# First stacks of an attention loaded inside the stage before it, its rows stored in wider transfers, and one instruction for the shift of a layer norm

## The chip, the cores and the metric

The kernel runs on one core of a Trainium2 chip. The metric is the time of one execution on the device in microseconds (us), the median of several runs. The engines are PE (matrix products), DVE (VectorE), ACT (ScalarE), POOL (GpSimd) and SP (SyncE, which here only issues transfers); each works through its own list of instructions in order and waits on semaphores for the others.

## The reference

Two transformer layers in float32 on a batch of two sequences of 1024 rows of width 512. Every part is `x = x + layernorm(part(layernorm(x)))`:

```python
x = x + _layernorm(_L0_attn_ref(_layernorm(x), Wq, Wk, Wv, Wo))   # 16 heads of 32, rotary, causal
x = x + _layernorm(_L0_ffn_ref(_layernorm(x), w_gate, w_up, w_down))        # silu(gate) * up, 2048 wide
x = x + _layernorm(_L1_attn_ref(_layernorm(x), ...))   # 16 heads, latent q (384) and kv (128), rotary on 64
x = x + _layernorm(_L1_ffn_ref(_layernorm(x), w_gate_up, w_proj))           # weights rounded to three values
```

The layer norm has no weights: `(x - m) / sqrt(v + eps)`. The kernel computes it as `x * rstd + shift` with `rstd = 1 / sqrt(v + eps)` and `shift = -m * rstd`.

## The kernel before

The work is a row of stages, each a block of its own whose engines all meet at its end. Tiles are 128 rows of width 512; there are 8 to a sequence and 16 in all. Most matrices are held as two float32r parts, a high one that ACT copies out of PSUM and a low one that DVE (or POOL) makes by subtraction.

`front_layer0` (line 698) is the first stage. It turns the three weights, normalises each tile, turns it, and multiplies it by the weights of q, k and v; the order of PE's, ACT's and DVE's work is written out by `front_order` (line 674). For q and k DVE's `rotate` (line 868) multiplies the PSUM bank by the cosines into `direct` and by the sines, crossed, into `crossed`; POOL adds the two into `turning` (line 923), PE turns that (line 808), and ACT and DVE write the two parts into `stage` (lines 840 and 901). For every two tiles SP's `store_pair` (line 753) writes `stage` to the DRAM tensor `qk_dram` in 16 transfers: two of q and k, two parts, four heads of a group, each from 32 partitions (line 760). The value rows go out tile by tile in one or two transfers of 128 partitions (lines 777 and 781).

`attention_layer0` (line 989) works head by head. For each head SP's `load_stack` (line 1027) reads `q_stack` and `k_stack`, three blocks of 32 partitions each (high, low, high for q; high, high, low for k) in four transfers, into a ring of four. The first three heads' loads are the first thing that SP does in the stage. PE's first product waits for `rows_set`, which DVE sets when it has written two rows of ones into each slot of `k_stack` (line 1193), and for the stack of head 0 (line 1127). In the first heads PE and DVE alternate: PE makes scores into `mbank` (line 1130), DVE takes their maxima (line 1209).

Four stages have layer norms with a shift: `project_residual_norm` (line 485, tag `l0o`, after the first attention), `residual_norm_and_weights` (line 2128, tag `w`), `latent_operands` for the second sequence (line 2421, tag `l1p`) and `residual_norm_transposed` (line 175, tag `f1n`). In the first, second and fourth DVE's `inverse` does, per tile and norm, a subtraction of the mean from `zero` into `minus`, a reciprocal of `std`, and the product of the two into `shift`, three instructions of 128x1. POOL adds the residual rows beside them, 128x512 from SBUF.

In `latent_operands` DVE's round for tile i ends with `bn_stats` of the rows (line 2619), then the three small instructions for the tile before (lines 2623, 2627 and 2630), then `bn_aggr` (line 2635). ACT's next round begins with the square root of that aggregate (line 2529), then the scaling of the tile before that (line 2534), then the copy of the projections out of PSUM (line 2541), on which DVE's round depends. POOL ends its round with a 1024-wide addition (line 2672).

What the front passes to the attention is laid out as

```python
qk_dram = dram("qk_dram", [B, 2, KT, GROUP_HEADS, 2, HD0, S])
```

## Time and profile before

| | |
|---|---|
| median of 3 runs | 3118.07 us (3117.04 to 3122.82) |
| the profiled execution | 3119.57 us |
| its span | 3117.8 us |
| mean granted PE clock | 0.958 |
| busy: PE, PEld, DVE, ACT, POOL | 2859.3, 2285.1, 1877.8, 1289.4, 1053.2 us |

The span is the time from the first to the last instruction of the profiled execution; a little lies around it. PE and PEld are the products and the weight loads of TensorE. A line such as L1130 is the line of the kernel that issued the instruction. In a timeline each row is an instruction or a few alike: start, duration, engine, line, what it writes and reads, and in brackets how long its engine stood idle before it and what ended that. The stages around the change: the front from 0 to 206 us, the first attention from there to 625, `project_residual_norm` 630 to 710, `residual_norm_and_weights` 1278 to 1376, `latent_operands` of the second sequence 2040 to 2129, `residual_norm_transposed` 2686 to 2731. The granted clock has two levels, 2.4 GHz (1.00 in the rows) and 1.2 GHz (0.50).

### The profile page before, as it was taken

The page shows a single profiled execution, that of the slowest core. Times are in us where ns is not written, and L with a number is a line of the kernel's source. Part 1 is how long each engine was busy: PE and PEld are TensorE (multiplying, and loading weights), DVE is VectorE, ACT ScalarE, POOL GpSimd, SP SyncE. Part 2 cuts the span into 40 slices and gives each one's busy share as a digit, 9 for nine tenths or more (in the row PEclk, how much of TensorE's full clock was granted, in tenths as well). Part 3 has the DMA queues.
Part 4 walks back from the last instruction along what each step waited for, and adds up shares of the span by engine and source line. Part 5 has one row for each costly group of instructions (what it writes and reads, how often), then busy time and mean ns, then how long its engine had stood idle before and what let it go on. Part 6 is the DMA issues. An engine that isn't in the chain of part 4 may idle for free. (4 is left out here: it accounts for less than half of the span.)

```text
span 3117.8 us, 43250 instructions
## 1 busy us (share of the span) xinstructions
PE 2859.3 (92%) x14636; PEld 2285.1 (73%) x14636; DVE 1877.8 (60%) x3698; ACT 1289.4 (41%) x2488; POOL 1053.2 (34%) x842
## 2 busy tenths in 40 slices
PE   7969999878999999688999999777999999599998
PEld 5846666557888888467888888666888888478886
DVE  5647888674544545635666666665666666744446
ACT  2216666653222222433444444333444444543335
POOL 1217877754645546414111111042111110132223
PEclk9979999988999999789999999899999999799999
DMA  4774444141121101570000000121000000200012
GB/s 163 235 225 133 128 131 128 54 149 63 53 80 49 62 25 36 183 271 16 13 18 12 12 18 3 77 81 35 12 18 12 12 12 4 101 21 21 10 37 81
DMA packets 136084, 217.87 MB, mean 70 GB/s; under 512 B 14512, under 2 KB 85168, under 8 KB 135440
## 3 DMA queue, kind: packets, MB, share of 16 engines
q1 hardware_dynamic: 135952, 216.19, 21.7%
q8 instruction: 73, 1.20, 0.2%
q14 instruction: 59, 0.48, 0.0%
HBM read 144.05 MB, written 71.83 MB: 69 GB/s over the span
## 5 line engine op out<-in xcount | busy, mean ns | idle before, releaser
L1525 ACT ACTIVATE l1a_probs<-l1a_scores,l1a_row 128x128 f32<-128x128 f32 (+7 forms) x256 | 189.4, 741 | 319.9 <-DVE l1a_row L1572 319.9
L1259 POOL TENSOR_TENSOR l0a_probs_hl<-l0a_probs,l0a_probs_hl 128x896 fp32r<-128x896 f32 (+1 forms) x128 | 284.9, 2245 | 107.4 <-ACT l0a_probs L1187 107.4
L1582 DVE TENSOR_TENSOR l1a_pT_hl<-l1a_work,l1a_pT_hl 128x512 fp32r<-128x512 f32 (+3 forms) x384 | 213.1, 555 | 170.1 <-ACT l1a_pT_hl L1532 169.9
L1499 PE MATMUL l1a_obank<-l1a_pT_hl,l1k_v_hl 128*128 128x512 f32 (+3 forms) x1152 | 300.3, 370 | 7.1 <-DVE l1a_pT_hl L1582 7.1
L1634 POOL TENSOR_TENSOR l1k_wabs<-l1a_wabs_raw,l1k_wabs 128x384 fp32r<-128x384 f32 x28 | 28.4, 1015 | 801.7 <-ACT l1k_wabs L1541 801.7
L1479 PE MATMUL l1a_scores<-l1k_kT_hl,l1a_qa_hl 128*128 128x512 f32 (+3 forms) x1152 | 290.8, 361 | 1.5 <-ACT l1a_probs L1525 1.5
L1507 PE MATMUL l1a_work<-l1a_wov,l1a_oT_hl 128*128 128x512 f32 x768 | 215.1, 403 | 5.0 <-DVE l1a_oT_hl L1601 3.0
L1532 ACT CAST l1a_pT_hl<-l1a_work 128x512 fp32r<-128x512 f32 (+3 forms) x384 | 183.5, 478 | 82.8 <-PE l1a_work L1490 81.5
L1572 DVE TENSOR_REDUCE l1a_row<-l1a_scores 128x1 f32<-128x128 f32 (+7 forms) x256 | 189.8, 751 | 44.0 <-PE l1a_scores L1482 43.9
L1596 DVE SCALAR_TENSOR_TENSOR l_acc<-l1a_work,l1a_row,l_acc 128x512 f32<-128x512 f32 x256 | 189.0, 748 | 27.1 <-PE l1a_work L1507 20.3
L1499 PEld LDWEIGHTS l1a_obank<-l1a_pT_hl,l1k_v_hl 128*128 128x128 f32 x1152 | 180.9, 191 | 33.3 <-DVE l1a_pT_hl L1582 14.8
L1479 PEld LDWEIGHTS l1a_scores<-l1k_kT_hl,l1a_qa_hl 128*128 128x128 f32 x1152 | 188.1, 190 | 21.7 <-ACT l1a_probs L1525 1.8
L1479 PE MATMUL l1a_scores<-l1k_kpe,l1a_q_stack 128*128 128x512 f32 (+3 forms) x768 | 203.0, 345 | 0.0
L1490 PE MATMUL l1a_work<-all_ident,l1a_probs 128*128 128x128 f32 x1152 | 191.4, 275 | 9.4 <-DVE l1a_qa_hl L1587 6.1
L1905 PE MATMUL f0f_gbank<-x_xT,f0f_wT 128*128 128x512 f32 x768 | 192.0, 399 | 1.4 <-DVE f0f_wT L1985 1.4
L1915 PE MATMUL f0f_ybank<-f0f_wT,f0f_h_hl 128*128 128x512 f32 x768 | 190.2, 396 | 0.1
L1905 PE MATMUL f0f_ubank<-x_xT,f0f_wT 128*128 128x512 f32 x768 | 189.4, 395 | 0.0
L1991 DVE TENSOR_TENSOR f0f_hid<-f0f_silu,f0f_ubank 128x512 f32<-128x512 f32 x64 | 44.0, 688 | 229.8 <-PE f0f_ubank L1905 212.3
L1186 ACT ACTIVATE l0a_probs_hl<-l0a_sbank 128x896 fp32r<-128x896 f32 (+1 forms) x128 | 124.4, 972 | 134.8 <-PE l0a_sbank L1152 77.6
L1490 PEld LDWEIGHTS l1a_work<-all_ident,l1a_probs 128*128 128x128 f32 x1152 | 139.7, 140 | 47.4 <-DVE l1a_qa_hl L1587 12.6
L2078 POOL TENSOR_TENSOR f1x_squares<-f1x_squares,f1f_sq 128x512 f32<-128x512 f32 x64 | 82.8, 1294 | 268.7 <-ACT f1f_sq L1950 268.7
L1905 PEld LDWEIGHTS f0f_gbank<-x_xT,f0f_wT 128*128 128x128 f32 x768 | 145.5, 190 | 36.8 <-DVE f0f_wT L1985 1.8
(283 smaller groups left out, 6416.3 us busy)
## 6 DMA issues: line engine op xcount, KB each, us to landing
v_dram<-l0f_v_rows SPq DMA_DIRECT2D x24, 768.0 KB, 4.0
qk_dram<-l0f_stage SPq DMA_DIRECT2D x128, 128.0 KB, 2.5
l0a_v_stage<-v_dram SPq DMA_DIRECT2D x32, 384.0 KB, 4.5
l0a_q_stack<-qk_dram SPq DMA_DIRECT2D x32, 256.0 KB, 3.5
l0a_k_stack<-qk_dram SPq DMA_DIRECT2D x32, 256.0 KB, 4.0
f0f_chunk<-in_L_ffn_w_gate_up SPq DMA_DIRECT2D x32, 256.0 KB, 2.6
l1a_wov_raw<-wov_dram SPq DMA_DIRECT2D x32, 256.0 KB, 2.7
l0a_v_stage<-v_dram SPq DMA_DIRECT2D x8, 768.0 KB, 6.4
```

Source lines behind the costliest of these rows:

```text
L1259: nc.gpsimd.tensor_tensor(probs_hl[:, r, 1, 0:wide], probs[:, r, 0:wide], f32(probs_hl[:, r, 0, 0:wide]), ALU.subtract).then_inc(low_done, 1)
L1479: last = pe.matmul(scores[:, buf, cols], lhs, rhs, start=(i == 0), stop=(not diagonal and i == len(steps) - 1))
L1490: last = pe.transpose(work[:, slot, i * P:(i + 1) * P], probs[s][:, first + n, :], ident[:, :])
L1499: last = pe.matmul(obank[:, c:SPAN], src["v_hl"][:, a, n, :], pT_hl[:, ring(n, s), b, c:SPAN], start=(n == 0 and i == 0), stop=(n == QT * ...
L1507: last = pe.matmul(work[:, slot, :], oT_hl[:, s, a, n * P:(n + 1) * P], wov[:, hp, b, :], start=(i == 0), stop=(i == 2))
L1525: nc.scalar.activation(probs[s][:, first:first + wide, :].rearrange("p k c -> p (k c)"), scores[:, n % S_AHEAD, 0:wide * P], ACT.Exp, bias ...
L1532: nc.scalar.copy(pT_hl[:, ring(n, s), 0, c:SPAN], work[:, slot, c:SPAN]).then_inc(turned_high, 1)
L1572: nc.vector.tensor_reduce(row[:, 0, row_slot:row_slot + 1], scores[:, n % S_AHEAD, 0:wide * P], AX.X, ALU.max, negate=True).then_inc(max_d ...
L1582: nc.vector.tensor_tensor(pT_hl[:, r, 1, c:SPAN], work[:, slot, c:SPAN], f32(pT_hl[:, r, 0, c:SPAN]), ALU.subtract).then_inc(work_free[slo ...
L1596: nc.vector.scalar_tensor_tensor(out=out[:, t, :], in0=work[:, slot, :], scalar=row[:, 2, row_slot:row_slot + 1], in1=out[:, t, :], op0=AL ...
L1905: last = pe.matmul(bank[:, b, :], wT[:, half, wa, w, c * HG + b * P:c * HG + (b + 1) * P], xT_hl[:, xa, c, a * SPAN:(a + 1) * SPAN], start ...
L1915: last = pe.matmul(ybank[:, b % 2, :], h_hl[:, a % 2, ht, ha, b * P:(b + 1) * P], wT[:, half, wa, 2, ht * D:(ht + 1) * D], start=(n == 0), ...
```

## The change

1. `qk_dram` is laid out with the part ahead of the head, and `store_pair` writes each of q and k and each part in one transfer from 128 partitions: 4 for a pair of tiles instead of 16.
2. The stacks are allocated outside both stages, over the place of the front's raw weights, as one tensor. `load_stack` becomes a function of its own with six transfers of 32 partitions for a head. The front's SP calls it for heads 0 to 2 after the value store of the second sequence's second tile, once the weights are turned and the first sequence's four pairs are stored. The attention's SP loads from head 3 on.
3. `direct` goes: `rotate` writes into `turning`, waiting for the transposes of two tiles before (a wait that POOL had), and POOL adds in place.
4. In the three joins with `inverse` one `scalar_tensor_tensor` computes `shift = mean * -1 * rstd`; `minus`, `zero` and their semaphores go.
5. In `latent_operands` the negation and the product move from DVE to ACT, as two scaled copies of 128x1 ahead of the scaling.

```diff
+def load_stack(sp, qk_dram, stacks, h, loaded):
+    b, g, j = h // NH, h % NH // GROUP_HEADS, h % GROUP_HEADS
+    slot = h % STACKS
+    for w, parts in ((0, (0, 1, 0)), (1, (0, 0, 1))):
+        for n, part in enumerate(parts):
+            sp.dma_start(f32(stacks[n * HD0:(n + 1) * HD0, w, slot, :]), qk_dram[b, w, g, part, j]).then_inc(loaded[slot], 16)
...
                 for w in range(2):
                     for part in range(2):
-                        for j in range(GROUP_HEADS):
-                            sp.dma_start(qk_dram[b, w, :, j, part, :, cols].rearrange("g d s -> d g s"),
-                                         f32(stage[j * HD0:(j + 1) * HD0, pair % 2, w, part])).then_inc(qk_stored[pair % 2], 16)
+                        sp.dma_start(qk_dram[b, w, :, part, :, :, cols].rearrange("g j d s -> (j d) g s"),
+                                     f32(stage[:, pair % 2, w, part])).then_inc(qk_stored[pair % 2], 16)
...
                 if t % 2 == 0 and t > 0:
                     store_pair(t // 2 - 1)
+                if t == TB + 1:
+                    sp.wait_ge(turned, use["W", 3 * KT - 1] + 1)
+                    for i in range(2):
+                        sp.wait_ge(qk_stored[i], 16 * 4 * TB // 4)
+                    for h in range(STACKS - 1):
+                        load_stack(sp, qk_dram, stacks, h, stack_loaded)
...
-                nc.vector.tensor_tensor(direct[:, w, :].rearrange("p (h d) -> p h d", d=HALF0),
+                if t >= 2:
+                    dve.wait_ge(turned, use["QK"[w], t - 2] + 1)
+                nc.vector.tensor_tensor(turning[:, t % 2, w, :].rearrange("p (h d) -> p h d", d=HALF0),
...
                     pool.wait_ge(read[w], t + 1)
-                    if t >= 2:
-                        pool.wait_ge(turned, use["QK"[w], t - 2] + 1)
-                    nc.gpsimd.tensor_tensor(turning[:, t % 2, w, :], direct[:, w, :], crossed[:, w, :], ALU.add
+                    nc.gpsimd.tensor_tensor(turning[:, t % 2, w, :], turning[:, t % 2, w, :], crossed[:, w, :], ALU.add
...
-            for first in range(STACKS - 1):
-                load_stack(first)
...
-                        pe.wait_ge(stack_loaded[hs], 64 * (h // STACKS + 1))
+                        pe.wait_ge(stack_loaded[hs], 96 * (h // STACKS + 1))
...
             def inverse(which, t):
                 r = t % RING
-                dve.wait_ge(mv_done[which], t + 1)
-                nc.vector.tensor_tensor(minus[:, which, r:r + 1], zero[:, :], mv[:, which, r, 0:1], ALU.subtract
-                                        ).then_inc(minus_done[which], 1)
                 dve.wait_ge(std_done[which], t + 1)
                 nc.vector.reciprocal(rstd[:, which, r:r + 1], std[:, which, r:r + 1]).then_inc(rstd_done[which], 1)
-                dve.wait_ge(minus_done[which], t + 1)
                 dve.wait_ge(rstd_done[which], t + 1)
-                nc.vector.tensor_tensor(shift[:, which, r:r + 1], minus[:, which, r:r + 1], rstd[:, which, r:r + 1],
-                                        ALU.mult).then_inc(shift_done[which], 1)
+                nc.vector.scalar_tensor_tensor(out=shift[:, which, r:r + 1], in0=mv[:, which, r, 0:1], scalar=-1.0,
+                                               in1=rstd[:, which, r:r + 1], op0=ALU.mult, op1=ALU.mult
+                                               ).then_inc(shift_done[which], 1)
...
                     nc.scalar.activation(r_std[:, t % 2:t % 2 + 1], r_mv[:, t % 3, 1:2], ACT.Sqrt, bias=eps_ln[:, 0:1]
                                          ).then_inc(r_std_done, 1)
+                    wait(act, r_shift_done, t - 1)
+                    nc.scalar.activation(r_minus[:, t % 2:t % 2 + 1], r_mv[:, t % 3, 0:1], ACT.Copy, scale=-1.0
+                                         ).then_inc(r_minus_done, 1)
                 if rows is not None and i >= 2:
                     t = i - 2
+                    act.wait_ge(r_minus_done, t + 1)
+                    act.wait_ge(r_inv_done, t + 1)
+                    wait(act, r_z_done, t - 1)
+                    nc.scalar.activation(r_shift[:, t % 2:t % 2 + 1], r_minus[:, t % 2:t % 2 + 1], ACT.Copy,
+                                         scale=r_inv[:, t % 2:t % 2 + 1]).then_inc(r_shift_done, 1)
                     act.wait_ge(r_shift_done, t + 1)
...
                     t = i - 1
-                    dve.wait_ge(r_mv_done, t + 1)
-                    nc.vector.tensor_tensor(r_minus[:, t % 2:t % 2 + 1], zero[:, :], r_mv[:, t % 3, 0:1], ALU.subtract
-                                            ).then_inc(r_minus_done, 1)
                     dve.wait_ge(r_std_done, t + 1)
                     wait(dve, r_z_done, t - 1)
                     nc.vector.reciprocal(r_inv[:, t % 2:t % 2 + 1], r_std[:, t % 2:t % 2 + 1]).then_inc(r_inv_done, 1)
-                    dve.wait_ge(r_minus_done, t + 1)
-                    dve.wait_ge(r_inv_done, t + 1)
-                    nc.vector.tensor_tensor(r_shift[:, t % 2:t % 2 + 1], r_minus[:, t % 2:t % 2 + 1],
-                                            r_inv[:, t % 2:t % 2 + 1], ALU.mult).then_inc(r_shift_done, 1)
...
-            qk_dram = dram("qk_dram", [B, 2, KT, GROUP_HEADS, 2, HD0, S])
+            qk_dram = dram("qk_dram", [B, 2, KT, 2, GROUP_HEADS, HD0, S])
...
+            with phase("l0w") as w:
+                raw_in = w.sb("raw", [P, 3, KT, D], side="right")[:, :, :, :]
+            early = ExitStack()
+            stack_phase = early.enter_context(phase("l0s"))
+            stacks = stack_phase.sb("stacks", [P, 2, STACKS, S], F32R, side="right")[:, :, :, :]
```

## Rows read from the trace of the kernel before

**Rows 1.** Stretches: busy us per engine (instructions), PE clock, DMA share, GB/s.

```profile
181.00:185.00 4.00, 4.00 (x23) 3.37 (x21) 2.91 (x6) 1.07 (x2) 1.30 (x1) 1.00 1.03 366
185.00:192.00 7.00, 3.02 (x18) 2.38 (x16) 2.70 (x6) 2.05 (x4) 1.29 (x1) 0.96 0.96 262
...
198.00:205.00 7.00, 0.00 (x0) 0.00 (x0) 0.00 (x0) 0.00 (x0) 0.00 (x0) 0.50 0.92 258
```

**Rows 2.** Timeline, end of the front and start of the attention.

```profile
193.06 11.14 SPq L760 DMA_DIRECT2D qk_dram<-l0f_stage  x16
...
206.65 2.50 DVE L1193 CAST l0a_k_stack<-l0a_ones 2x1024 fp32r<-2x1024 f32 x4 [16.48 <-POOL l0a_ones L1243]
...
211.99 0.45 PE L1130 MATMUL l0a_mbank<-l0a_k_stack,l0a_q_stack 96*128 96x128 f32 x1 [23.97 <-DMA l0a_k_stack<-qk_dram]
```

**Rows 3.** Timeline, one round of `latent_operands`, second batch (start, duration, engine).

```profile
2058.59 0.68 DVE L2619 BATCH_NORM_STATS2 l1p_r_stats<-l_acc 128x6 f32<-128x512 f32 x1
...
2058.75 2.40 POOL L2672 TENSOR_TENSOR l1k_qpe<-l1k_qpe,l1p_crossed 128x1024 f32<-128x1024 f32 x1 [0.92 <-DVE l1p_crossed L2611]
...
2059.19 1.97 DVE L2623 TENSOR_TENSOR l1p_r_minus<-l1p_zero,l1p_r_mv 128x1 f32<-128x1 f32 x1
2061.08 0.15 DVE L2627 RECIPROCAL l1p_r_inv<-l1p_r_std 128x1 f32<-128x1 f32 x1
...
2061.41 0.17 DVE L2635 BATCH_NORM_AGGREGATE l1p_r_mv<-l1p_r_stats 128x2 f32<-128x6 f32 x1
2061.62 0.29 ACT L2529 ACTIVATE l1p_r_std<-l1p_r_mv,l1p_eps_ln 128x1 f32<-128x1 f32 x1 [6.36 <-DVE l1p_r_mv L2635]
2061.82 0.80 ACT L2534 ACTIVATE l_acc<-l_acc,l1p_r_shift,l1p_r_inv 128x512 f32<-128x512 f32 x1
...
2068.87 0.68 DVE L2619 BATCH_NORM_STATS2 l1p_r_stats<-l_acc 128x6 f32<-128x512 f32 x1
...
2081.91 0.79 DVE L2630 TENSOR_TENSOR l1p_r_shift<-l1p_r_minus,l1p_r_inv 128x1 f32<-128x1 f32 x1
```

**Rows 4.** Tile `l1p_r_minus`: its eight instructions, min/median/max ns.

```profile
L2623 DVE TENSOR_TENSOR l1p_r_minus<-l1p_zero,l1p_r_mv x8: 139/1970/1977, 2050.7 to 2120.6; 128x1 f32<-128x1 f32 x8
```

**Rows 5.** Stretches, `latent_operands`, a round in the middle.

```profile
2069.00:2079.00 10.00, 8.35 (x48) 7.22 (x48) 7.10 (x16) 4.24 (x13) 5.75 (x9) 1.00 0.14 51
```

**Rows 6.** Timeline, `latent_operands`, its last rounds.

```profile
2111.51 6.75 PE L2517 MATMUL l1p_pbank<-l1x_wpT,l1k_qT_hl 128*128 128x512 f32 x18 [1.38 <-DVE l1p_crossed L2611]
```

**Rows 7.** Groups of DVE instructions, `project_residual_norm` (busy us, mean ns, idle before).

```profile
L631 DVE TENSOR_TENSOR l0o_shift<-l0o_minus,l0o_rstd 128x1 f32<-128x1 f32 x32 | 16.5, 516 | 3.3
L625 DVE TENSOR_TENSOR l0o_minus<-l0o_zero,l0o_mv 128x1 f32<-128x1 f32 x32 | 12.7, 396 | 0.0
```

**Rows 8.** Stretches, the middle of `project_residual_norm`.

```profile
668.00:684.00 16.00, 14.19 (x66) 10.81 (x67) 14.43 (x42) 11.80 (x27) 10.55 (x9) 1.00 0.40 133
```

**Rows 9.** Timeline, one tile of `project_residual_norm`.

```profile
672.77 0.64 DVE L625 TENSOR_TENSOR l0o_minus<-l0o_zero,l0o_mv 128x1 f32<-128x1 f32 x1
...
673.34 0.15 DVE L628 RECIPROCAL l0o_rstd<-l0o_std 128x1 f32<-128x1 f32 x1
673.60 0.16 DVE L631 TENSOR_TENSOR l0o_shift<-l0o_minus,l0o_rstd 128x1 f32<-128x1 f32 x1
```

**Rows 10.** Timeline, `residual_norm_transposed`, one tile.

```profile
2722.43 0.14 DVE L238 TENSOR_TENSOR f1n_minus<-f1n_zero,f1n_mv 128x1 f32<-128x1 f32 x1
2722.48 0.16 DVE L241 RECIPROCAL f1n_rstd<-f1n_std 128x1 f32<-128x1 f32 x1
```

**Rows 11.** Groups of DVE instructions, the other two joins.

```profile
L2373 DVE TENSOR_TENSOR w_minus<-w_zero,w_mv 128x1 f32<-128x1 f32 x24 | 7.5, 314 | 0.0
...
L238 DVE TENSOR_TENSOR f1n_minus<-f1n_zero,f1n_mv 128x1 f32<-128x1 f32 x24 | 4.2, 176 | 0.0
```

**Rows 12.** Groups of ACT instructions: one table load.

```profile
L2313 ACT ACT_TABLE_LOAD x1 | 1.3, 1283 | 9.6 <-DVE w_mv L2368 9.6
```

**Rows 13.** Stretches, the attention before and after the clock rises.

```profile
240.00:260.00 20.00, 19.64 (x103) 13.26 (x101) 14.97 (x30) 12.26 (x15) 12.03 (x6) 0.93 0.53 157
```

More of the change, by code:

```diff
@@ L183, in residual_norm_transposed @@
     stats, mv = m.sb("stats", [P, 2, RING, 6]), m.sb("mv", [P, 2, RING, 2])
-    std, rstd, minus, shift = (m.sb(n, [P, 2, RING]) for n in ("std", "rstd", "minus", "shift"))
-    zero = m.sb("zero", [P, 1])
+    std, rstd, shift = (m.sb(n, [P, 2, RING]) for n in ("std", "rstd", "shift"))
     eps = m.sb("eps", [P, 1])
@@ L496, in project_residual_norm @@
     stats, mv = m.sb("stats", [P, 2, RING, 6]), m.sb("mv", [P, 2, RING, 2])
-    std, rstd, minus, shift = (m.sb(n, [P, 2, RING]) for n in ("std", "rstd", "minus", "shift"))
-    zero = m.sb("zero", [P, 1])
+    std, rstd, shift = (m.sb(n, [P, 2, RING]) for n in ("std", "rstd", "shift"))
     eps = m.sb("eps", [P, 1])
@@ L707, in front_layer0 @@
     cos, sin = m.sb("cos", [P, 2, TB, HALF0]), m.sb("sin", [P, 2, TB, 2, HALF0])
-    direct, crossed = m.sb("direct", [P, 2, D]), m.sb("crossed", [P, 2, D])
+    crossed = m.sb("crossed", [P, 2, D])
     turning = m.sb("turning", [P, 2, 2, D])
@@ L986, in uses_layer0, with attention_layer0 @@
     return out
-def attention_layer0(nc, m, ident, ident_bf, mask, qk_dram, v_dram, v32_dram, sums_dram, inverse_dram, out, next_load):
+def attention_layer0(nc, m, ident, ident_bf, mask, qk_dram, v_dram, v32_dram, sums_dram, inverse_dram, out, next_load, stacks,
+                     stack_loaded):
     mbank = m.ps("mbank", [P, 2, SPAN])
@@ L999, in attention_layer0 @@
     negmax_hl = m.sb("negmax_hl", [TB, 2, 2, P], F32R)
-    q_stack, k_stack = (m.sb(n, [P, STACKS, S], F32R) for n in ("q_stack", "k_stack"))
+    q_stack, k_stack = stacks[:, 0], stacks[:, 1]
     v_stage = m.sb("v_stage", [P, 2, TB, GROUP_HEADS, 3 * HD0], F32R)
@@ L1006, in attention_layer0 @@
     ones = m.sb("ones", [P, 1])
-    stack_loaded = [m.sem(f"stack_loaded{i}") for i in range(STACKS)]
     v_loaded = [m.sem(f"v_loaded{i}") for i in range(2)]
@@ L2136, in residual_norm_and_weights @@
     stats, mv = m.sb("stats", [P, 2, RING, 6]), m.sb("mv", [P, 2, RING, 2])
-    std, rstd, minus, shift = (m.sb(n, [P, 2, RING]) for n in ("std", "rstd", "minus", "shift"))
-    zero = m.sb("zero", [P, 1])
+    std, rstd, shift = (m.sb(n, [P, 2, RING]) for n in ("std", "rstd", "shift"))
     eps = m.sb("eps", [P, 1])
```

71 lines of the change are left out of this document (24 added, 47 removed).

## The prediction, made before the changed kernel was run

> **What bounds the kernel now.** I read the windows first, because the kernel is a row of stages with different limits, then the timeline around each place that the diff touches, then the groups of DVE instructions.
>
> The end of the front is bound by transfers. In the last stretches the DMA engines are 92 to 103% busy; they move 366 GB/s where the value rows (128 partitions, 1.5 KB pieces) lead, and 258 to 262 GB/s where the rotated rows (32 partitions, 1 KB pieces) lead [rows 1]. The sixteen stores of the last pair are issued from 193.06 to 204.2, and the next stage issues its first load only after they landed, at 206.5. DVE then writes the ones rows until 209.15, and PE starts at 211.99, released by the key stack's load [rows 2].
>
> The second batch's `latent_operands` is one serial loop over DVE and ACT, 10.28 us a round (2058.59 to 2068.87, both the same statistics). In it DVE's 128x1 subtraction at L2623 takes 1.97 us where the undisturbed takes 0.14 [rows 3, 4], because POOL's 1024-wide addition, started at 2058.75, runs until 2061.15; the next statistics' aggregate stands behind it, and ACT stood idle for 6.36 us until that aggregate [rows 3]. The median of the eight is 1970 ns, the shortest 139 [rows 4]: six are long. PE works 8.35 of 10 us there, so it is not the bound [rows 5].
>
> `project_residual_norm` is bound by DVE from about 655 on (14.43 of 16 us busy, PE 14.19) [rows 8]. Its 128x1 subtractions and multiplications average 396 and 516 ns [rows 7], three times the undisturbed 130 to 160.
>
> **Part 1: stores in a quarter of the transfers.** From 181.0 to 205.6 the queue carries four value stores of 786 KB and two pairs of 2.10 MB: 3.15 MB at 366 GB/s is 8.6 us and 4.19 MB at 260 is 16.1, together 24.7, which is the measured stretch. Bytes and piece sizes stay. SP's issue shrinks from 11.14 us for 16 [rows 2] to four instructions, but that alone gives little, as the engines are 92 to 96% busy. What can change is the rate of a transfer that spans 128 partitions. If it stays at 260 the gain is 0; if it reaches the 366 of the value rows it is 16.1 - 11.5 = 4.6 us. A loss is not excluded by a row, but a wider transfer of the same pieces has no reason for more than 1 us. I take 2.0, nearer to the lower end, since the pieces stay 1 KB. The other seven pairs are hidden under PE, which is full there.
>
> The Trainium skill (SBUF — State Buffer, "Door 1: The DMA port swizzle") says that 32 neighbouring partitions reach only 8 of 16 DMA ports, half of 435 GB/s. The rows show more than that half, 258 to 262, so neighbouring transfers must overlap; by the page's limit for HBM, 358 GB/s, this part would be an estimated 4.4 us and the sum 3096.5.
>
> **Part 2: three stacks loaded inside the front.** The wait of PE from 209.15 to 211.99 goes, 2.8 us; late next are the ones rows (2.50 us of DVE, from 206.65), which stay [rows 2]. The 18 loads (2.36 MB) are issued after the ninth tile's value store. At 260 to 366 GB/s they take 6.4 to 9.1 us of queue; at the stores' 11.14 / 16 = 0.70 us each [rows 2] SP issues them in 12.5 us. The next value store comes 9.5 us after, so it is some 3 us late, and the two-deep value and stage buffers give a whole tile more before ACT would notice. I cost that at 0; if the cover fails, ACT and then PE wait some 2 us. Later heads issue six loads instead of four, 1.4 us more of SP per head, behind nothing that PE waits for: 0. The clock was at half level from 192 and reads 0.93 in the 20 us from 240 [rows 13]; I assume that its rise moves with PE's restart.
>
> **Part 3: `direct` becomes `turning`.** DVE now waits for a transpose of two tiles before, done a whole tile (9.5 us) earlier in PE's written order. POOL's addition is the same size in place. 0.
>
> **Part 4: shifts in `latent_operands`.** DVE loses L2623 and L2630. The aggregate can then start as soon as the statistics end, at about 2059.3 instead of 2061.41: 2.1 us. ACT gains two 128x1 activations ahead of the scaling. The one of that size costs 0.20 us to the next instruction and 0.29 in full [rows 3]; the second must be complete before the scaling reads it, so 0.20 + 0.35 = 0.55. Net 1.55 a round. The round becomes 8.7 us, just above PE's work of 8.35 x 1.03 = 8.6 [rows 5], so PE does not yet eat it. Of the six long ones the last is off the path: the matmul group at 2111.51, at low clock for 6.75 us, ends after it [rows 6]. Five rounds give 7.75; in two of them the multiplication too is held, 0.79 against 0.16 us [rows 3], 1.3 more; the first rounds, with nothing held, pay 0.4. Sum: 8.6. Bounds: 5 if PE's order binds first, and 11 if PE's shorter pause keeps the clock up, which saves 6.75 - 4.34 = 2.4.
>
> **Part 5: one instruction for two in the other joins.** Undisturbed, the removed instruction delays the next by only 0.05 to 0.06 us [rows 10], since small ones follow closely. Where it is held, the remaining two-input instruction is held until the same moment, and what is saved is the reciprocal's latency, now under the hold: 673.60 - 673.34 = 0.26 [rows 9]. In `project_residual_norm`, of the 26 from 655 on nine are held for over 0.5 us (one of them is in [rows 9]): 9 x 0.25 + 17 x 0.06 = 3.2 us. In `residual_norm_transposed` 24 x 0.06 = 1.4, and one of them held: 1.6. In the join before the second layer the mean is 314 ns [rows 11], six held in the DVE-bound half, 2.0; half of it is lost as loads follow: 1.0. Bounds for the three together: 1 us (the tiles fall into a worse pattern against POOL) and 13.
>
> **Sum.** 2.0 + 2.8 + 8.6 + 3.2 + 1.6 + 1.0 = 19.2. The profiled execution took 3119.6 (its span is 3117.8, 1.8 lie around it), so it would be 3100.4; the median of the runs is 1.5 below that execution, so I say 3099. About 0.2%, 6 us, is what a measurement can tell from no change.
>
> **Rivals.**
> A, the new form is not held by POOL. No row shows a three-operand instruction with both inputs in SBUF beside a long POOL addition. If it runs free, `project_residual_norm` loses nearly all of 16.5 + 12.7 us of small work less 32 x 0.16, until PE's 14.19 of 16 binds [rows 7, 8]: 6 us instead of 3.2; the other two give 4 more; with the clock kept up (2.4) the time is 3090. For: the lengths come from the hold alone. Against: inputs are what is shared, and they are the same two. The Trainium skill (SBUF — State Buffer, "Who interferes with whom") says that a DVE instruction with two SBUF inputs contends with a GpSimd instruction that reads SBUF, whatever its operation; by that rule the forecast stands.
> B, the gains shrink in their loops: PE's written order caps the round (5 us), the joins fall into another beat with POOL (1), the stores keep their rate (0), only 2.8 is whole. 3109.
> C, the change doesn't pay: the scaled copies on ACT need another function table than the square root. One load is 1.283 us [rows 12]; two a round for eight rounds are 20.5 us on ACT's path, 3120, no change. Against: the weights' stage uses a scaled copy between its roots and the next, with no load.
> D, slower: the attention's first heads, where PE waits for DVE's maxima, keep the clock at half level longer. A mean of 0.93 over the 20 us from 240 puts the rise at about 243; PE then works 19.64 of 20 us [rows 13], so each us at half level costs half a us. The gain of 19 and 6 more are eaten if the rise comes 50 us later against the work, after 290: 3124. For: the rise needs some activity, and the start is moved. Against: the same instructions follow in the same order.
>
> **Chances.** Forecast 0.60, A 0.16, B 0.14, C 0.07, D 0.03. Faster: forecast, A and B, 0.90; same 0.07; slower 0.03. The low end takes A and the upper bounds of parts 1 and 4, 3086; the high end is B with a us on top, 3110.
>
> **What would show it.** The first matmul of the attention at about 207.1, behind the ones rows. The last store landing near 204. No L2623-like row on DVE; aggregates 8.7 us apart in `latent_operands`, and its ACT with two more 128x1 activations and no table load. The shift rows still with lengths of 1.0 to 1.2 us in `project_residual_norm`, which ends 3 us shorter. It is wrong if those lengths vanish (A), if PE idles in the front after 142, if PE's rows touch one another in `latent_operands` at more than 9 us a round (B), or if the granted clock stays at half level past 290 (D).

## The result and the profile after

The changed kernel takes 3087.82 us in the median (3083.03 to 3089.88, four runs) where the kernel before takes 3119.2 (3117.04 to 3122.82, four runs): a ratio of 0.9896, 95% interval 0.9879 to 0.9913, 31.4 us less. The profiled execution took 3087.36 us, its span 3085.6. Forecast were 3099 and a range of 3086 to 3110.

The start of each stage shows where the 32.2 us of the span went. "Offset" is a stage's first start after less before.

| | before | after | offset | gained in the stage before it, forecast |
|---|---|---|---|---|
| first product of the attention (`l0a_mbank`) | 212.0 | 206.8 | -5.2 | 5.2, forecast 4.8 |
| `project_residual_norm` (`l0o_tbank`) | 630.3 | 624.0 | -6.3 | 1.1, none |
| first feed-forward (`f0f_gbank`) | 720.7 | 702.6 | -18.1 | **11.8, forecast 3.2** |
| `latent_operands`, first sequence (`l1p_dbank`) | 1376.8 | 1354.0 | -22.8 | 4.7, forecast 1.0 |
| turns ahead of its second sequence (`l1n_bank`) | 2022.9 | 2001.8 | -21.1 | -1.7, none |
| last product of that sequence (`l1p_pbank`, last start) | 2124.8 | 2093.8 | -31.0 | 9.9, forecast 8.6 |
| second feed-forward (`f1f_gbank`) | 2736.2 | 2703.5 | -32.7 | 1.7, forecast 1.6 |

The page of the changed kernel, busy times and instructions. DVE lost 100 instructions and 28.8 us, ACT gained 16 and 5.0:

```profile
PE 2855.0 (93%) x14636; PEld 2285.4 (74%) x14636; DVE 1849.0 (60%) x3598; ACT 1294.4 (42%) x2504; POOL 1054.3 (34%) x842
```

Timeline of the changed kernel, end of the front and start of the attention, to be held against [rows 2]. SP issues four stores in 5.56 us, the next block begins at 204.13 in place of 206.52, and PE is released by the ones rows, with no wait for a stack:

```profile
192.03 5.56 SPq L753 DMA_DIRECT2D qk_dram<-l0f_stage  x4
204.13 0.10 POOL L1234 MEMSET l0a_ones<- 128x1 f32 x1 [15.67 <-POOLq L740]
...
204.26 2.50 DVE L1184 CAST l0s_stacks<-l0a_ones 2x1024 fp32r<-2x1024 f32 x4 [12.81 <-POOL l0a_ones L1234]
...
206.82 0.47 PE L1121 MATMUL l0a_mbank<-l0s_stacks 96*128 96x128 f32 x1 [17.52 <-DVE l0s_stacks L1184]
```

The same stretches as [rows 1]. From 185 on 344 GB/s stand where 262 stood, and the last stretch is no longer full. The stretch from 192 is led by the value rows (262 of its 356 GB/s), so the last line shows four microseconds in which the new stores move alone:

```profile
181.00:185.00 4.00, 4.00 (x23) 3.40 (x22) 2.71 (x6) 1.08 (x2) 1.30 (x1) 1.00 0.74 259
185.00:192.00 7.00, 4.29 (x24) 3.41 (x22) 3.24 (x6) 2.05 (x4) 1.29 (x1) 1.00 1.04 344
192.00:198.00 6.00, 0.00 (x0) 0.00 (x0) 0.00 (x0) 0.00 (x0) 0.00 (x0) 0.67 1.03 356
198.00:205.00 7.00, 0.00 (x0) 0.00 (x0) 0.74 (x2) 0.87 (x1) 0.10 (x1) 0.50 0.76 251
...
198.00:202.00 4.00, 0.00 (x0) 0.00 (x0) 0.00 (x0) 0.00 (x0) 0.00 (x0) 0.50 1.04 344
```

One round of `latent_operands`, second sequence, against [rows 3]. From one statistics to the next it is 8.62 us in place of 10.28. The aggregate comes 0.72 us after the statistics begin, where it came 2.82 after, and ACT's two new instructions stand between root and scaling. From the statistics to the scaling it is 1.54 us in place of 3.23, and the 1.69 between them are, to a few hundredths, the 1.66 that the round lost:

```profile
2037.77 0.68 DVE L2608 BATCH_NORM_STATS2 l1p_r_stats<-l_acc 128x6 f32<-128x512 f32 x1
...
2037.93 2.40 POOL L2654 TENSOR_TENSOR l1k_qpe<-l1k_qpe,l1p_crossed 128x1024 f32<-128x1024 f32 x1 [0.93 <-DVE l1p_crossed L2600]
...
2038.37 0.14 DVE L2613 RECIPROCAL l1p_r_inv<-l1p_r_std 128x1 f32<-128x1 f32 x1
2038.49 0.18 DVE L2617 BATCH_NORM_AGGREGATE l1p_r_mv<-l1p_r_stats 128x2 f32<-128x6 f32 x1
2038.70 0.30 ACT L2512 ACTIVATE l1p_r_std<-l1p_r_mv,l1p_eps_ln 128x1 f32<-128x1 f32 x1 [4.26 <-DVE l1p_r_mv L2617]
2038.91 0.19 ACT L2515 ACTIVATE l1p_r_minus<-l1p_r_mv 128x1 f32<-128x1 f32 x1
2039.00 0.28 ACT L2522 ACTIVATE l1p_r_shift<-l1p_r_minus,l1p_r_inv 128x1 f32<-128x1 f32 x1
2039.31 0.82 ACT L2525 ACTIVATE l_acc<-l_acc,l1p_r_shift,l1p_r_inv 128x512 f32<-128x512 f32 x1
2040.04 0.62 ACT L2532 COPY l1p_down<-l1p_dbank 128x576 f32<-128x576 f32 x1
...
2046.39 0.68 DVE L2608 BATCH_NORM_STATS2 l1p_r_stats<-l_acc 128x6 f32<-128x512 f32 x1
```

The groups of DVE in `project_residual_norm`, against [rows 7]. The new instruction is as long as the two-input ones were, so it is still held by POOL; but there are 32 of it in place of 64:

```profile
L616 DVE SCALAR_TENSOR_TENSOR l0o_shift<-l0o_mv,l0o_rstd 128x1 f32<-128x1 f32 x32 | 17.7, 552 | 1.1
```

### The profile page after: what moved, and what is told of

Same layout as the page of the kernel before. It is cut to its first block and busy times, and to the rows that moved or that the text cites. A ratio compares the mean times of both kernels' runs of the same rounds, so it can differ in the third digit from the quotient of the medians.

```text
span 3085.6 us, 43025 instructions
## 1 busy us (share of the span) xinstructions
PE 2855.0 (93%) x14636; PEld 2285.4 (74%) x14636; DVE 1849.0 (60%) x3598; ACT 1294.4 (42%) x2504; POOL 1054.3 (34%) x842
## 5 line engine op out<-in xcount | busy, mean ns | idle before, releaser
L1490 PEld LDWEIGHTS l1a_obank<-l1a_pT_hl,l1k_v_hl 128*128 128x128 f32 x1152 | 181.2, 191 | 33.2 <-DVE l1a_pT_hl L1573 14.8
L1481 PEld LDWEIGHTS l1a_work<-all_ident,l1a_probs 128*128 128x128 f32 x1152 | 140.5, 141 | 47.7 <-DVE l1a_qa_hl L1578 12.7
```

What stands on the lines that cost most here:

```text
L1481: last = pe.transpose(work[:, slot, i * P:(i + 1) * P], probs[s][:, first + n, :], ident[:, :])
L1490: last = pe.matmul(obank[:, c:SPAN], src["v_hl"][:, a, n, :], pT_hl[:, ring(n, s), b, c:SPAN], start=(n == 0 and i == 0), stop=(n == QT * ...
```

## The experiments

Eleven kernels and the changed one again, in three groups, each group on one chip beside the kernel before (3121.4, 3124.3 and 3117.8 us there). Intervals of a ratio are some 0.0015 to either side, 4 to 5 us, so a part is read in its stage, where most rulers repeat themselves to a few tenths of a us. The length of `project_residual_norm` runs from its first turn to the first product of the feed-forward (90.4 us before, 78.6 after), that of the weights' join from the last product ahead of it (`f0f_ybank`) to the first of `latent_operands`, that of the transposed join from the last `l1a_work` to the first `f1f_gbank`. "The changed kernel" is 3087.82 above. `before`, from here on, is the profile shown ahead of the prediction.

### 1. The big term: one instruction for two in `project_residual_norm`

**Three instructions again, the negation with two inputs.** In the changed kernel, that stage alone:

```diff
+                dve.wait_ge(mv_done[which], t + 1)
+                nc.vector.tensor_tensor(minus[:, which, r:r + 1], zero[:, :], mv[:, which, r, 0:1], ALU.subtract
+                                        ).then_inc(minus_done[which], 1)
...
-                nc.vector.scalar_tensor_tensor(out=shift[:, which, r:r + 1], in0=mv[:, which, r, 0:1], scalar=-1.0,
-                                               in1=rstd[:, which, r:r + 1], op0=ALU.mult, op1=ALU.mult
-                                               ).then_inc(shift_done[which], 1)
+                dve.wait_ge(minus_done[which], t + 1)
+                nc.vector.tensor_tensor(shift[:, which, r:r + 1], minus[:, which, r:r + 1], rstd[:, which, r:r + 1],
+                                        ALU.mult).then_inc(shift_done[which], 1)
```

> The changed kernel with the three instructions put back in project_residual_norm alone (subtraction from zero, reciprocal, product). Theory H (each of the two instructions with two SBUF inputs can be held by a POOL addition of its own, so the form before was held up to twice a norm and the new form once): the stage from its first turn to the first product of the feed-forward takes its 90.4 us of before again instead of 78.6, and the whole is 11 to 12 us slower than the changed kernel, about 3099. Theory P (the 11.8 us come from where the stage now falls against the clock and the loads, not from the form): the stage stays under 82 us and the whole within 3 us of the changed kernel, about 3088 to 3091.

Measured: 3091.91 us (3089.88 to 3095.25), ratio 0.9906 [0.9889, 0.9922]. The stage takes 87.1 us, 8.5 more than the changed kernel's 78.6 and 3.3 less than the 90.4 of before. The stage goes most of the way that theory H foretold, and no cause was sought for the rest. The whole is 4.1 us slower than the changed kernel where H had 11 to 12, and the two intervals overlap, so H rests on the stage alone. How a norm is held twice shows in its timeline:

```profile
648.27 1.28 POOL L663 TENSOR_TENSOR l0o_z<-l0o_z,l0o_x 128x512 f32<-128x512 f32 x1 [1.18 <-ACT l0o_z L562]
...
648.62 0.16 DVE L613 BATCH_NORM_AGGREGATE l0o_mv<-l0o_stats 128x2 f32<-128x6 f32 x1
648.71 0.87 DVE L618 TENSOR_TENSOR l0o_minus<-l0o_zero,l0o_mv 128x1 f32<-128x1 f32 x1
...
649.50 0.15 DVE L621 RECIPROCAL l0o_rstd<-l0o_std 128x1 f32<-128x1 f32 x1
649.51 1.29 POOL L656 TENSOR_TENSOR l0o_ot_hl<-l_oT,l0o_ot_hl 128x512 fp32r<-128x512 f32 x1
...
649.68 1.14 DVE L624 TENSOR_TENSOR l0o_shift<-l0o_minus,l0o_rstd 128x1 f32<-128x1 f32 x1
...
650.74 0.17 DVE L613 BATCH_NORM_AGGREGATE l0o_mv<-l0o_stats 128x2 f32<-128x6 f32 x1
```

The negation starts at 648.71 beside POOL's addition (648.27 to 649.55) and ends with it. By the time that the reciprocal is done, POOL has begun its next addition (649.51), and the product is held by that one for 1.14 us. The next aggregate comes 2.12 us after the last. So the two are not held "until the same moment", as the prediction had it, but by two additions in turn. Both instructions of one norm are held (over 0.25 us each) in 8 of the 32 norms here, and in 4 in `before`. The changed kernel's same rounds, one hold to a norm:

```profile
643.26 1.29 POOL L656 TENSOR_TENSOR l0o_z<-l0o_z,l0o_x 128x512 f32<-128x512 f32 x1
643.67 0.17 DVE L609 BATCH_NORM_AGGREGATE l0o_mv<-l0o_stats 128x2 f32<-128x6 f32 x1
643.75 0.13 DVE L614 RECIPROCAL l0o_rstd<-l0o_std 128x1 f32<-128x1 f32 x1
...
643.92 0.65 DVE L616 SCALAR_TENSOR_TENSOR l0o_shift<-l0o_mv,l0o_rstd 128x1 f32<-128x1 f32 x1
644.50 0.17 DVE L609 BATCH_NORM_AGGREGATE l0o_mv<-l0o_stats 128x2 f32<-128x6 f32 x1
644.52 1.29 POOL L649 TENSOR_TENSOR l0o_ot_hl<-l_oT,l0o_ot_hl 128x512 fp32r<-128x512 f32 x1
...
645.76 1.29 POOL L656 TENSOR_TENSOR l0o_z<-l0o_z,l0o_x 128x512 f32<-128x512 f32 x1
...
647.01 1.29 POOL L649 TENSOR_TENSOR l0o_ot_hl<-l_oT,l0o_ot_hl 128x512 fp32r<-128x512 f32 x1
```

From aggregate to aggregate it is 0.83 us. And POOL starts each addition at the end of the last, from 643.26 to 647.01: a round of 2.50 is its two additions. With two holds POOL waits for ACT's scaled tile 1.18 us of each round, which is the 3.72.

In `before` the later rounds, those of 4.25 us, differ: no norm is held twice, but the two norms of a round have one hold each. The negation of one is held to the end of POOL's addition into `l0o_ot_hl` (0.64 us, the norm of [rows 9]); the product of the other starts just behind POOL's next residual addition and is held for 1.15:

```profile
675.11 1.29 POOL L670 TENSOR_TENSOR l0o_z<-l0o_z,l0o_x 128x512 f32<-128x512 f32 x1 [1.71 <-ACT l0o_z L569]
675.26 1.15 DVE L631 TENSOR_TENSOR l0o_shift<-l0o_minus,l0o_rstd 128x1 f32<-128x1 f32 x1
```

In the changed kernel's rounds of 2.8 and 3.0 us that product is ahead of the addition and runs free, and the one hold left is of 0.46 us:

```profile
667.17 0.16 DVE L616 SCALAR_TENSOR_TENSOR l0o_shift<-l0o_mv,l0o_rstd 128x1 f32<-128x1 f32 x1
...
667.25 1.29 POOL L656 TENSOR_TENSOR l0o_z<-l0o_z,l0o_x 128x512 f32<-128x512 f32 x1 [0.21 <-ACT l0o_z L560]
...
668.11 0.46 DVE L616 SCALAR_TENSOR_TENSOR l0o_shift<-l0o_mv,l0o_rstd 128x1 f32<-128x1 f32 x1
```

**Three instructions, the negation with one input.** As above, but

```diff
-                nc.vector.tensor_tensor(minus[:, which, r:r + 1], zero[:, :], mv[:, which, r, 0:1], ALU.subtract
+                nc.vector.tensor_scalar(minus[:, which, r:r + 1], mv[:, which, r, 0:1], -1.0, None, ALU.mult
```

> As the run before, three instructions in project_residual_norm, but the negation reads one tensor only (mean times -1); the product keeps its two. Theory H: the negation is never held (120 to 160 ns each), the product is held as the new form is, and the stage takes 79 to 81 us (32 instructions of some 0.05 us more than the changed kernel): about 3088 to 3090. Rival C (what counts is the number of DVE instructions and their handshakes in the chain, not the holds): the stage takes about 90 us again, about 3099.

Measured: 3087.50 us (3084.02 to 3089.38), ratio 0.9890 [0.9873, 0.9906]; the stage takes 80.1 us, 7.0 less than with the two-input negation. With as many instructions as before it is as fast as the changed kernel, so rival C falls: it is the hold that costs, not the instruction. Tile `l0o_minus` of this kernel and of the one above (min/median/max ns, first and last start):

```profile
L614 DVE TENSOR_SCALAR l0o_minus<-l0o_mv x32: 113/119/145, 639.0 to 691.8; 128x1 f32<-128x1 f32 x32
```
```profile
L618 DVE TENSOR_TENSOR l0o_minus<-l0o_zero,l0o_mv x32: 120/148/1243, 635.5 to 696.7; 128x1 f32<-128x1 f32 x32
```

**The new form in the kernel before, in that stage alone.**

> The kernel before with only project_residual_norm's shift made by the one new instruction. Theory H (up to two holds a norm become one, and the beat of the rounds falls): 8 to 11 us faster, 3110 to 3112 where the kernel before is 3120, the first rounds at 2.5 us in place of 3.72 and the later ones at 2.9 in place of 4.25. The prediction's step (only the reciprocal's latency is saved): 3 us, 3117. Rival S (the stage gained by what came before it, a sooner or later start against the clock and the loads): 0 to 3 us, 3117 to 3120.

Measured: 3108.35 us (3106.06 to 3113.03, seven runs), ratio 0.9969 [0.9958, 0.9981], that is 9.7 us of 3118. The stage takes 78.5 us. Theory H's forecast of 8 to 11 us is met, the prediction's 3 us are refuted. The stage's clearest ruler is POOL's residual addition, one a tile, with its first and last start, in this kernel and then in the one with three instructions again and both held:

```profile
L663 POOL TENSOR_TENSOR l0o_z<-l0o_z,l0o_x x16: 1262/1288/1299, 646.8 to 693.6; 128x512 f32<-128x512 f32 x16
```
```profile
L663 POOL TENSOR_TENSOR l0o_z<-l0o_z,l0o_x x16: 1264/1284/1299, 637.1 to 692.1; 128x512 f32<-128x512 f32 x16
```

46.8 us for the 15 rounds with one hold (46.9 and 46.8 in two runs of the changed kernel, 47.0 with the one-input negation); 55.0 with two, and 56.5 in `before`. There most rounds are 3.72 or 4.25 us; with one hold most are 2.50, or later 2.8 and 3.0 in turn.

### 2. Does a scalar pointer count as an input?

**The shift of all three joins from one tensor.** In the changed kernel:

```diff
-                nc.vector.scalar_tensor_tensor(out=shift[:, which, r:r + 1], in0=mv[:, which, r, 0:1], scalar=-1.0,
-                                               in1=rstd[:, which, r:r + 1], op0=ALU.mult, op1=ALU.mult
-                                               ).then_inc(shift_done[which], 1)
+                nc.vector.tensor_scalar(shift[:, which, r:r + 1], mv[:, which, r, 0:1], rstd[:, which, r:r + 1], -1.0,
+                                        ALU.mult, ALU.mult).then_inc(shift_done[which], 1)
```

> The changed kernel with the shift in the three joins computed from one tensor input and a per-partition scalar (mean * rstd * -1), rstd read as the scalar. Theory H with 'a scalar pointer is not a second input': no shift instruction is over 0.3 us; the three joins lose 17.7 + 7.5 + 9.7 us of DVE less 80 x 0.16, that is 22 us busy, of which project_residual_norm gives 5 to 8 (DVE 13.4 of 14 us busy there, PE 13.9, so PE binds soon), the weights' join 1 to 3 and the transposed one 1 to 3: 3074 to 3081. Rival R (the scalar pointer is read over the same port and is held alike): the lengths stay at 1.0 to 1.2 us and the time at 3087 to 3089.

Measured: 3080.01 us (3077.94 to 3083.11), ratio 0.9870 [0.9854, 0.9887], 7.8 us below the changed kernel. Not one is held: 28 of the stage's 32 run beside an instruction of POOL, and all take 212 to 215 ns:

```profile
L615 DVE TENSOR_SCALAR l0o_shift<-l0o_mv,l0o_rstd x32: 212/214/215, 636.1 to 687.0; 128x1 f32<-128x1 f32 x32
```
```profile
L603 DVE BATCH_NORM_STATS2 l0o_stats<-l0o_ybank 128x6 f32<-128x512 f32 x16 | 11.2, 699 | 16.2 <-PE l0o_ybank L534 16.2
```

The gain is not where the expectation put most of it. `project_residual_norm` takes 77.0 us, 1.6 less, not 5 to 8, though DVE is rid of 10.9 us of work: it now waits 16.2 us for PE's product (7.6 in the changed kernel), so DVE has ceased to bind. The transposed join takes 47.9 us (51.1), 3.2 less, with seven holds of over 0.5 us gone, and 47.5 to 47.8 in the three later kernels with this form. The weights' join takes 92.4 us (95.8 in the changed kernel), but 93.0 to 95.6 in those three, where seven profiles with the held form have 94.9 to 97.9, so its gain is not firm.

**The same for `latent_operands`.** On top of that, the two activations leave ACT and DVE makes the shift behind its reciprocal:

```diff
-                    nc.scalar.activation(r_minus[:, t % 2:t % 2 + 1], r_mv[:, t % 3, 0:1], ACT.Copy, scale=-1.0
-                                         ).then_inc(r_minus_done, 1)
...
-                    nc.scalar.activation(r_shift[:, t % 2:t % 2 + 1], r_minus[:, t % 2:t % 2 + 1], ACT.Copy,
-                                         scale=r_inv[:, t % 2:t % 2 + 1]).then_inc(r_shift_done, 1)
...
+                    dve.wait_ge(r_inv_done, t + 1)
+                    nc.vector.tensor_scalar(r_shift[:, t % 2:t % 2 + 1], r_mv[:, t % 3, 0:1], r_inv[:, t % 2:t % 2 + 1], -1.0,
+                                            ALU.mult, ALU.mult).then_inc(r_shift_done, 1)
```

> As joins_pointer (3080.0), and in latent_operands the shift too is made on DVE from one tensor and a scalar pointer, in place of the two activations on ACT. Theory A (the loop stays serial over DVE and ACT, so what leaves ACT's path is gained): ACT loses 0.55 us and DVE gains 0.06 to 0.15 a round, rounds of 8.2 us, the whole 2 to 3 us faster, 3077. Rival B (PE, busy 19.17 of 20 us in these rounds, binds): rounds stay at 8.5 to 8.6 and the time within 1 us of 3080.

Measured: 3077.07 us (3071.68 to 3082.03), ratio 0.9854 [0.9837, 0.9872]. Rounds of 8.34 to 8.37 us, between the two theories: 0.25 less. It is theory A with its prices put right. From the statistics' start to ACT's copy of the projections (`l1p_down`) it is 2.27 us in the changed kernel's rows above and 2.02 here, since ACT's path from the root to that copy lost 0.43 and the aggregate came 0.19 later; the round is shorter by just that 0.25.

### 3. `latent_operands` alone

**The kernel before with the second sequence's shifts on ACT**, the stage's part of the change and nothing else.

> The kernel before with latent_operands of the changed one, nothing else. Theory of the prediction (the subtraction held by POOL's 1024-wide addition stands in a serial loop of DVE and ACT): rounds of 8.6 us in place of 10.3, the whole 8 to 10 us faster, 3109 to 3112. Rival (those 9.9 us of the changed trace came in part from where the stage falls against clock and loads): 3 to 6 us, 3114 to 3117.

Measured: 3112.92 us (3108.63 to 3116.08, seven runs), ratio 0.9969 [0.9958, 0.9980], 9.7 us of 3124. From the second statistics to the eighth it takes 51.6 us, 51.9 in the changed kernel, 61.15 in `before` and 61.1 in the kernel of section 1 that leaves this stage alone: 9.3 us for the part, forecast 8.6. The rounds of 10.3 became 8.6, those of 10.9 8.6 to 8.9, and the first, where nothing was held, went from 8.46 to 8.6.

**The aggregate ahead of the reciprocal.** The kernel with all pointers and the early ones rows (below), and in `latent_operands` `bn_aggr` moved ahead of the reciprocal and the shift.

> As all_pointer_ones, and in latent_operands the aggregate, on which ACT's next root waits, stands ahead of the reciprocal and the shift on DVE. Theory S (the loop is still serial): rounds of 8.1 to 8.2 us in place of 8.37, 1.5 us less. Rival B (PE, 19.65 of 20 us busy with 8.37, has 8.22 of work a round and binds): rounds of 8.2 to 8.35, at most 1 us less.

Measured: 3072.87 us (3070.01 to 3075.59), ratio 0.9855 [0.9840, 0.9870]; rounds of 8.20 to 8.35 us, mostly 8.31. The number is rival B's, its reason is not: the aggregate comes 0.20 us sooner, but the scaling now waits for the shift, and ACT's copy begins 1.96 us after the statistics in place of 2.02, the same 0.06 that the round lost. PE is nearly full all the same, 19.17 of 20 us in the changed kernel and 19.65 with the pointers, so little is left here:

```profile
2040.00:2060.00 20.00, 19.17 (x112) 16.89 (x111) 11.84 (x32) 11.55 (x40) 13.85 (x24) 1.00 0.17 53
```
```profile
2040.00:2060.00 20.00, 19.65 (x115) 17.16 (x114) 13.43 (x36) 10.01 (x29) 15.16 (x21) 1.00 0.24 80
```

### 4. The seam between front and attention

The ruler here is PE's idle time between the front's last transpose and the attention's first product: 23.97 us in [rows 2], 17.52 in the changed kernel's row above, and 17.49 to 17.55 in five other runs with that front (24.78 and 25.11 in the two kernels of the experiments that keep the front of before).

**Sixteen stores again**, stacks still loaded in the front:

```diff
-                        sp.dma_start(qk_dram[b, w, :, part, :, :, cols].rearrange("g j d s -> (j d) g s"),
-                                     f32(stage[:, pair % 2, w, part])).then_inc(qk_stored[pair % 2], 16)
+                        for j in range(GROUP_HEADS):
+                            sp.dma_start(qk_dram[b, w, :, part, j, :, cols].rearrange("g d s -> d g s"),
+                                         f32(stage[j * HD0:(j + 1) * HD0, pair % 2, w, part])).then_inc(qk_stored[pair % 2], 16)
```

> The changed kernel with each store of rotated rows split into four again (16 transfers of 32 partitions for a pair), stacks still loaded in the front. Theory W (a transfer over 128 partitions moves faster than four over 32): 262 GB/s instead of 344 to 356 in the last stretches, the next stage begins 2 to 4 us later, first attention product at 209 to 211, the whole 2 to 4 us slower than the changed kernel, 3090 to 3092. Rival I (the gain was in the loads' place or in the order of the queue, not in the width): rate and time as in the changed kernel, 3087 to 3088.

Measured: 3092.42 us (3090.07 to 3093.86), ratio 0.9900 [0.9885, 0.9915]; PE stands idle for 21.05 us, 3.5 more. Theory W: the same bytes in the same 1 KB pieces move at 268 and 272 GB/s from 32 partitions, 258 and 262 in [rows 1], and at 344 from 128. The edit changes two things together, how many partitions a transfer spans and how many transfers there are, and no run tells these apart.

```profile
185.00:192.00 7.00, 3.84 (x22) 3.04 (x20) 3.24 (x6) 2.05 (x4) 1.29 (x1) 1.00 0.98 272
192.00:198.00 6.00, 0.00 (x0) 0.00 (x0) 0.00 (x0) 0.00 (x0) 0.00 (x0) 0.62 1.01 335
198.00:205.00 7.00, 0.00 (x0) 0.00 (x0) 0.00 (x0) 0.00 (x0) 0.00 (x0) 0.50 0.95 268
```

The stretch from 192 has 335 GB/s since the value rows fall into it.

**The stacks at the start of the attention again.** The front's loads are dropped and the attention's SP begins with

```diff
+            for first in range(STACKS - 1):
+                load_stack(sp, qk_dram, stacks, first, stack_loaded)
```

> The changed kernel with the first three heads' stacks loaded at the start of the attention again (18 transfers). Theory of the prediction: PE waits for the stack of head 0 some 2.8 us behind the ones rows and starts 5.3 to 6 us after the block's start, the whole 2.8 us slower, 3090 to 3091. Rival (a front without 2.36 MB of loads in its middle runs its own stores sooner, and the two cancel): the last store lands 1 us sooner and the whole is within 1.5 us of the changed kernel.

Measured: 3090.82 us (3087.69 to 3092.48), ratio 0.9894 [0.9879, 0.9909]; PE stands idle for 20.87 us, 3.35 more, and is released by the load, as in [rows 2]:

```profile
203.04 0.10 POOL L1230 MEMSET l0a_ones<- 128x1 f32 x1 [15.60 <-POOLq L740]
...
203.17 2.51 DVE L1180 CAST l0s_stacks<-l0a_ones 2x1024 fp32r<-2x1024 f32 x4 [12.74 <-POOL l0a_ones L1230]
203.35 8.29 SPq L690 DMA_DIRECT2D l0s_stacks<-qk_dram  x18
...
209.15 0.44 PE L1117 MATMUL l0a_mbank<-l0s_stacks 96*128 96x128 f32 x1 [20.87 <-DMA l0s_stacks<-qk_dram]
```

The 18 loads in the front cost its PE nothing: from 142 to 182 PE is busy for 40.00 of 40 us in the changed kernel, SP issues them from 133.99 in 9.72 us (forecast 12.5), and the next value store follows at 143.75. The rival's 1 us is not seen; the next block begins 14.8 us after PE's end with the loads and without them, and the front's last product ends at 188.24 us in the second run of the changed kernel and at 188.28 here.

**The ones rows in the front.** DVE writes them at the end of `front_layer0`, and the attention's own go with their semaphores:

```diff
+            for slot in range(STACKS):
+                nc.vector.tensor_copy(stacks[QW:KW, 1, slot, :], ones[QW:KW, :].to_broadcast([2, S]))
...
-            pe.wait_ge(rows_set, 1)
```

> The changed kernel with the rows of ones written into the key stacks by DVE at the end of the front, while the last stores land, instead of at the start of the attention. Theory of the prediction (after the stacks' wait is gone, these 2.5 us of DVE are what PE waits for): the first attention product comes 2.5 us sooner, at about 204.3, and the whole is 2.5 us faster, about 3085. Rival (something else then ends last: the block's own start on PE, or the clock's rise, which comes at its own time after the pause): PE starts sooner, but the whole is within 1 us of the changed kernel, 3087 to 3088.

Measured: 3084.96 us (3083.86 to 3087.48), ratio 0.9883 [0.9867, 0.9900]. PE is idle for 14.84 us in place of 17.5: the 2.7 us are there at the first product. In the whole, 2.5 us are less than the runs can tell.

**All pointers and the early ones rows together.**

> All four shifts from one tensor and a scalar pointer, and the rows of ones written in the front. Additive: the ones rows gave 2.5 us at the first attention product and 2.5 in the medians (3087.5 to 3085.0), so 3074.5 with all_pointer at 3077.1. Rival (the sooner start meets a later clock rise, as the spans of ones_early suggest, -33.6 against -32.2): 3076.

Measured: 3074.01 us (3069.99 to 3076.97), ratio 0.9856 [0.9841, 0.9871]. The idle time is 14.9 us again, so the gain is there; the ratio is that of the pointers alone (0.9854), so the whole leaves it open.

**The changed kernel once more**, on the chip of the last three.

> The changed kernel itself, once more beside the kernel before on the chip of this call, as the measure for the others and for how far each stage's length moves by itself. In the kernel with only latent_operands changed, whose first 2040 us are the kernel before, the stages' starts stood at +1.4, +2.2, +0.9, +1.1 and -1.8 us against the profile before. Expected: a ratio of 0.989 to 0.991, project_residual_norm 76 to 80 us long as in the changed kernel's first profile (78.6).

Measured: 3085.89 us (3083.54 to 3087.08), ratio 0.9895 [0.9880, 0.9910]; `project_residual_norm` 79.9 us. Beside it the best version (all pointers, early ones rows, aggregate first) is 13.0 us faster, 3072.87, its interval [0.9840, 0.9870] apart from that of the changed kernel. It beats both kernels.

## Why the prediction was right, and where it was off

The sign held, and three of the six terms were shown by runs of their own: the stores, the stack wait and `latent_operands`. The smaller joins have no run that takes one of them alone. The gain forecast, 19.2 us, was 12 short, and that 3087.82 lies inside the range is in part luck. The low end, 3086, was set for rival A, whose mechanism is false, and its sum does not come out: A's 9.2 us and the stores' upper 2.6 under the forecast are 3087.2, or 3084.8 if the clock's 2.4 is counted a second time with part 4.

The parts by their own rulers, forecast beside them:

| | forecast (bounds) | shown | by |
|---|---|---|---|
| stores from 128 partitions | 2.0 (0 to 4.6) | 3.5 | idle time of PE, narrow stores |
| no wait for the stacks | 2.8 | 2.8 to 3.4 | idle time of PE, late stacks |
| shifts on ACT in `latent_operands` | 8.6 (5 to 11) | 9.3 to 9.6 | six rounds, in the changed kernel and that part alone |
| `project_residual_norm` | 3.2 | 8.2 to 9.7 | fifteen rounds, that part alone and undone |
| transposed join | 1.6 | 1.9 | stage 51.1 to 51.2 us in seven profiles, 52.8 to 53.4 in three |
| weights' join | 1.0 | some 2, not clear of drift | stage 94.9 to 97.9 us in seven profiles, 97.5 to 100.5 in three |

Together these are 28 to 30 of the 31.4 us; what is left is less than the whole can tell.

**The term that failed** is the one for `project_residual_norm`. The prediction counted nine long rows and priced each at 0.25 us, since "the remaining two-input instruction is held until the same moment". In [rows 9] the product is indeed not held by another addition, and I took that norm for all. But four norms, the last at 660.8 us, were held by two of POOL's additions in turn, and in the later rounds the product of the round's other norm was held by the next addition, for 1.15 us. Taking the negation's hold away alone gave 7.0 us (80.1 for 87.1), where nine times 0.25 is 2.3. The row that says it was at hand: the two sums in [rows 7], 12.7 and 16.5 us, are together 19.9 above the 64 x 0.145 of undisturbed ones, and after the change 17.7 less 32 x 0.16 is 12.6. The difference of 7.3 and the instructions' own cost, 32 x 0.06 = 1.9, make 9.2 us, close to the 9.7 that the part alone gave. That they meet is no proof, since the sum after is known only from the changed kernel. Had the term been "one of two holds goes", [rows 7] bounded it: the negations alone are 12.7 us where 32 x 0.14 are undisturbed, 8.2 more. (The recorded 3.2 is also 3.3 by its own terms, 2.25 and 1.02.)

**PE's room** was misjudged with it. From "14.19 of 16 us busy" [rows 8] rival A's gain was capped at 6 us. In the kernel with the new form here alone PE counts 80 products in such a stretch, in 15.90 us, where [rows 8] has 66 in 14.19:

```profile
670.00:686.00 16.00, 15.90 (x80) 13.01 (x79) 15.34 (x50) 13.70 (x30) 11.65 (x10) 1.00 0.43 148
```

That is 0.199 us of busy time each in place of 0.215. The spans of single products are as before (medians 0.39 us for 128x512 and 0.27 for 128x128, in both kernels); fed closer together they overlap more, so a busy share below the full understates the room.

**The stores** reached the upper part of their bounds. I took the lower end because the pieces stay at 1 KB; the runs show that with the same pieces the wider and fewer transfers are faster. The Trainium skill (SBUF — State Buffer, "Door 1: The DMA port swizzle") offers a reason, that 32 neighbouring partitions reach half the ports; the trace agrees in direction and not in size, 258 to 272 GB/s from 32 partitions where half of its 435 is 218.

**The stack wait and `latent_operands`** came as worked out: first product at 206.82 (207.1 foretold), the next block at 204.13 (the last landing foretold near 204), rounds of 8.62 us (8.7), no table load, ACT's new instructions 188 and 282 ns. Part 3 was put at nothing and has no run of its own; PE is full from 142 to 182 us. The Trainium skill (SBUF — State Buffer, "Who interferes with whom") was right against rival A: an instruction with two inputs in SBUF is held whatever its operation (up to 1173 ns), and one with a single input is not (145 ns at most).

**The rivals.** A's time, 3090, was nearer than the forecast, but its mechanism is false: the shift rows are as long as before. B (the round capped by PE's order above 9 us, the stores at their old rate) is refuted by rounds of 8.62 us and 344 GB/s. C is refuted by the kernel with only that part, 9.7 us faster. D did not happen: the first 20 us of the attention are at 0.50 in both kernels, and the stretch from 235 to 255 is at 1.00 in the changed kernel where it is at 0.81 in `before`.

**What is not from the change.** The front's compute ended 1.3 us later in the changed kernel: 24 products from 34.7 took 8.44 us where they took 7.27, at an otherwise equal start. The second run of the changed kernel has 0.2 in place of the 1.3. In the kernel that alters only `latent_operands`, whose first 2040 us are the kernel before, stages move by up to 2.5 us against `before` (first attention product +1.4, `project_residual_norm` 89.1 us for 90.4, the weights' join 98.0 for 100.5). So of the 4.7 us in the weights' join half or more may be drift. The 1.1 us gained and 1.7 lost in the two attentions are inside what the same code does by itself: over the fourteen profiles the first takes 417.2 to 419.7 us and the stretch with the second 644.7 to 649.0, with no order by the kernel. `before`'s own stages were on the long side, which adds to the trace's difference.

## What to carry to other kernels

Where a small instruction on DVE is several times longer than its shortest, sum what all of them are above that shortest, and ask for each in turn which POOL instruction ends with it: two in one serial step, or in one round, can be held by two different ones, and taking one away can then give a whole hold a round. Better than fewer such instructions is none: a per-partition operand read as a scalar pointer was not held in any of these joins. A store that leaves from 128 partitions at once is worth having where the transfer ends a stage.

## What the runs showed of the hardware that I had not expected

- A `tensor_scalar` with its per-partition operand in SBUF takes 212 to 216 ns in all 80 cases of the three joins, 51 of which run beside an instruction of POOL, while the two-input form there takes 159 to 1244.
- The same bytes and pieces leave SBUF at 258 to 272 GB/s in many transfers of 32 partitions and at 344 in a quarter as many of 128.
- A loop that is held once a round repeated itself to 0.2 us over 15 rounds in seven profiles (46.8 to 47.0); held twice, it took 55.0 or 56.5, its rounds up to 5.5 us apart.
- With no hold left, `project_residual_norm` settled at 3.2 us a round, longer than the 2.9 with one hold, and yet ended sooner since its first rounds were shorter. What sets the 3.2 was not tried.
